# A graph network on one core: extra tiles tested ahead of the group, register words loaded early, dense product in four parts

## What is computed

```python
h = relu(layernorm(x))
# three graph convolutions, edges and self loops, norm = dinv[src] * dinv[dst]
for W, b in ((W1, b1), (W2, b2), (W3, b3)):
    h = segment_sum((h @ W)[src] * norm, dst) + b     # relu after the first two
x = x + h
h = relu(layernorm(x))
filt = edge_attr_50 @ W_rad.T + b_rad
x = x + silu(segment_sum((h @ W_pre.T + b_pre)[src] * filt, dst) @ W_post.T + b_post)
```

## Time and profile before

| | us |
|---|---|
| median of 3 runs | 6268.11 (6235.98 to 6292.54) |
| profiled execution, its own time | 6264.8 |
| its span, first to last instruction | 6263.0 |
| mean granted TensorE clock | 0.803 |

### The profile page before, as it was taken

The page is one execution under the profiler, slowest core; times in us unless marked ns, Lnnn a source line. Parts: engine busy times, 40 slices in busy tenths (PEclk is TensorE's granted clock), DMA queues, the critical chain, the costliest instruction groups (busy, mean ns, idle before and its releaser), DMA issues.

```text
span 6263.0 us, 114127 instructions
## 1 busy us (share of the span) xinstructions
PE 4667.6 (75%) x31388; PEld 3424.1 (55%) x31389; DVE 3181.7 (51%) x8799; ACT 951.1 (15%) x2182; POOL 2930.3 (47%) x3027
## 2 busy tenths in 40 slices
PE   6955787888888888599975999656666666666665
PEld 4741233444444445588855888455555555555555
DVE  6757777777766665544445444362222222222225
ACT  0010123333334554100001000010000000000002
POOL 0002123344440000276653766517777777777772
PEclk9967899999999999699967999666666666666665
DMA  1000011111121111255522555302222222222221
GB/s 32 0 15 13 27 41 43 55 55 56 56 66 52 52 63 53 71 168 168 173 55 71 168 169 175 77 29 47 47 46 47 47 46 47 46 47 46 47 47 33
DMA packets 158567, 406.28 MB, mean 65 GB/s; under 512 B 67564, under 2 KB 80940, under 8 KB 139124
## 3 DMA queue, kind: packets, MB, share of 16 engines
q1 hardware_dynamic: 62068, 305.32, 13.7%
q0 software_dynamic: 96256, 98.76, 8.5%
HBM read 307.53 MB, written 96.33 MB: 64 GB/s over the span
## 4 chain that ended last, share of the span: by engine, by line
PE 36%; POOL 25%; issue 18%; DVE 13%; DVEq 7%; DMA 1%; ACT 0%; SPq 0%; POOLq 0%; ACTq 0%
POOL rows_flat L508 25%; PE ps L1251 13%; PE ps L1343 5%; PE ps L1317 5%; PE ps L1223 4%; DVE sumT L961 4%; PE ps L1354 3%; PE ps L1240 3%; PE ps L1238 2%; DVE stage_fn L689 1%; PE ps L1209 1%; DVE hot L683 1%; DVEq L689 1%; DVEq L712 1%; DVE hot L1189 1%
## 5 line engine op out<-in xcount | busy, mean ns | idle before, releaser
L508 POOL DMA_INDIRECT rows_flat<-table,row_stage x3008 | 2917.2, 970 | 2136.9 <-issue 1844.2
L1231 PE MATMUL ps<-hot,msg_flat 128*64 128x160 f32 x3136 | 814.2, 447 | 711.2 <-DVE msg_flat L785 711.2
L1343 PE MATMUL ps<-sumT,stage_fn 128*128 128x392 f16 x3976 | 980.4, 358 | 418.1 <-DVE sumT L961 234.4
L1231 PEld LDWEIGHTS ps<-hot,msg_flat 128*64 128x64 f32 x3136 | 653.7, 216 | 827.0 <-issue 703.4
L961 DVE TENSOR_SCALAR sumT<-stage_fn,sub_start,sumT 128x784 f16<-128x784 f16 x1988 | 891.5, 481 | 0.0
L1343 PEld LDWEIGHTS ps<-sumT,stage_fn 128*128 128x128 f16 x3976 | 287.8, 101 | 1086.6 <-issue 829.4
L585 ACT ACTIVATE ring<-ps 128x784 fp8e4<-128x784 f32 x800 | 658.5, 823 | 1255.5 <-PE ps L1343 1250.0
L1251 PE MATMUL ps<-wide,ring 128*128 128x192 bf16 x9800 | 828.5, 247 | 0.0
L1251 PEld LDWEIGHTS ps<-wide,ring 128*128 128x128 fp8e4 x9800 | 805.7, 98 | 8.5
L683 DVE TENSOR_SCALAR hot<-iota,dst_rel 128x160 f32<-128x160 f32 (+1 forms) x3008 | 636.1, 287 | 226.7 <-issue 223.4
L785 DVE TENSOR_TENSOR msg_flat<-rows_flat,ps 128x512 f32<-128x512 f32 x196 | 134.6, 687 | 1007.1 <-DMA rows_flat<-table,row_stage 988.9
(11 more groups left out here) (160 smaller groups left out, 3071.1 us busy)
## 6 DMA issues: line engine op xcount, KB each, us to landing
ring<-counts SPq DMA_DIRECT2D x100, 1568.0 KB
counts<-ring SPq DMA_DIRECT2D x50, 1568.0 KB, 5.2
rows_flat<-table,row_stage POOLq DMA_INDIRECT x3008
ring<-in_radial SPq DMA_DIRECT2D x196, 200.0 KB
table<-node SPq DMA_DIRECT2D x56, 224.0 KB, 1.9
out<-node SPq DMA_DIRECT2D x13, 224.0 KB
ring<-in_dst SPq DMA_DIRECT2D x1, 784.0 KB
ring<-in_src SPq DMA_DIRECT2D x1, 784.0 KB
```

Source lines behind the costliest of these rows:

```text
L508: nc.gpsimd.indirect_dma_start(out=rows[:, j, k * D:(k + 1) * D], out_offset=None, in_=table[:, :], in_offset=bass.IndirectOffsetOnAxis(ap ...
L1231: s = nc.tensor.matmul(to, of, mats[:, k, :], start=(k == 0), stop=(k == BLOCK_TILES - 1))
L1343: m = nc.tensor.matmul(to[:, c, :], sources[:, :, k], joint[k][:, c * (JOINT // 2):(c + 1) * (JOINT // 2)], start=first, stop=True, skip_g ...
```

## The change

In `subs` the test for extra tiles moves ahead of the group. On DVE both tests now lie inside one `If(n > 0)`. On PE `If(n > 0)` comes ahead of the set's waits and matmuls; its true branch has the main tiles with the extra ones between them, its else branch has the main tiles alone, four matmuls in a row. The words t0 and n of four sets lie side by side in one table, so that DVE loads eight words at once and PE four; the load for the next group is issued ahead of the group's last set, and the first group's before the loop. The table has eight words more at its end, set to zero. PE's inner loop of two is written out, and the dense product is cut into four parts (25, 25, 24 and 24 matmuls), one behind each call of `subs`.

```diff
-        sub_tile = sbuf("sub_tile", [1, SUBS], I32)
-        sub_more = sbuf("sub_more", [1, SUBS], I32)
+        sub_table = sbuf("sub_table", [1, 2 * (SUBS + SETS)], I32)
+        by_sets = sub_table[:, 0:2 * SUBS].rearrange("a (s two k) -> a s two k", two=2, k=SETS)
+        sub_tile, sub_more = by_sets[:, :, 0, :], by_sets[:, :, 1, :]
...
+            nc.gpsimd.memset(sub_table[:, 2 * SUBS:], 0).then_inc(consts_made, 1)
...
             def subs(s4):
-                dve.load(tile_regs, sub_tile[0:1, bass.ds(s4 * SETS, SETS)])
-                dve.load(more_regs, sub_more[0:1, bass.ds(s4 * SETS, SETS)])
                 for a in range(SETS):
                     sub = s4 * SETS + a
                     t0 = counted(tile_regs[a], EDGES // P)
                     n = counted(more_regs[a], TILES // EXTRA)
+                    if a == SETS - 1:
+
+                        dve.load(tile_regs + more_regs, sub_table[0:1, bass.ds((s4 + 1) * (2 * SETS), 2 * SETS)])
 
                     dve.wait_ge(main_used, s4 * SETS + (a + 1))
...
-                    with dve.If(n > 1):
-                        with dve.Fori(0, n >> 1) as m2:
-                            for b in range(2):
-                                extra_hots(b, sub, extra_tile(t0, m2 * 2 + b))
-                    with dve.If((n & 1) > 0):
-                        extra_hots(0, sub, extra_tile(t0, n - 1))
+                    with dve.If(n > 0):
+                        with dve.If(n > 1):
+                            with dve.Fori(0, n >> 1) as m2:
+                                for b in range(2):
+                                    extra_hots(b, sub, extra_tile(t0, m2 * 2 + b))
+                        with dve.If((n & 1) > 0):
+                            extra_hots(0, sub, extra_tile(t0, n - 1))
...
+            dve.load(tile_regs + more_regs, sub_table[0:1, 0:2 * SETS])
             build_and_first_layer()
...
+            cuts = [0, 25, 50, 74, WINDOWS]
+
             def dense_part(i, h, part):
...
-                for q in range(part * (WINDOWS // 2), (part + 1) * (WINDOWS // 2)):
+                for q in range(cuts[part], cuts[part + 1]):
...
-                if part == 1:
+                if part == 3:
                     d.then_inc(dense_ready, 1)
...
             def subs(s4):
-                pe.load(more_regs, sub_more[0:1, bass.ds(s4 * SETS, SETS)])
                 for a in range(SETS):
...
+                    if a == SETS - 1:
+
+                        pe.load(more_regs, sub_table[0:1, bass.ds((s4 + 1) * (2 * SETS) + SETS, SETS)])
                     to = ps_count[a % 2]
-                    pe.wait_ge(sub_copied, s4 * SETS + (a + 1))
-                    pe.wait_ge(main_ready, s4 * SETS + (a + 1))
-                    pe.sem_inc(pe_turn, 1)
-                    for k in range(MAIN - 1):
-                        joint_tile(to, src_main[a], joint_main[a], k, k == 0)
-                    with pe.If(n > 1):
-                        with pe.Fori(0, n >> 1):
-                            for b in range(2):
-                                extra_tiles(to, b)
-                    with pe.If((n & 1) > 0):
-                        extra_tiles(to, 0)
-                    joint_tile(to, src_main[a], joint_main[a], MAIN - 1, False).then_inc(main_used, 1)
+
+                    def main_begins():
+                        pe.wait_ge(sub_copied, s4 * SETS + (a + 1))
+                        pe.wait_ge(main_ready, s4 * SETS + (a + 1))
+                        pe.sem_inc(pe_turn, 1)
+                        for k in range(MAIN - 1):
+                            joint_tile(to, src_main[a], joint_main[a], k, k == 0)
+
+                    def main_ends():
+                        joint_tile(to, src_main[a], joint_main[a], MAIN - 1, False).then_inc(main_used, 1)
+
+                    with pe.If(n > 0):
+                        main_begins()
+                        with pe.If(n > 1):
+                            with pe.Fori(0, n >> 1):
+                                for b in range(2):
+                                    extra_tiles(to, b)
+                        with pe.If((n & 1) > 0):
+                            extra_tiles(to, 0)
+                        main_ends()
+                    with pe.Else():
+                        main_begins()
+                        main_ends()
 
             def build_and_first_layer():
                 at = Pass(pe, FUSED)
                 with pe.Fori(0, PAIRS) as i:
                     for j in range(SLOTS):
-                        with pe.Fori(0, P // SUB // SETS // 2) as q:
-                            subs(i * (2 * P // SUB // SETS) + j * (P // SUB // SETS // 2) + q)
-                        if j < 2:
-                            with pe.If(i > 0):
-                                dense_part(earlier(i), 1, j)
-                        else:
-                            dense_part(i, 0, j - 2)
+                        for q in range(2):
+                            subs(i * (2 * P // SUB // SETS) + (j * 2 + q))
+                            if j < 2:
+                                with pe.If(i > 0):
+                                    dense_part(earlier(i), 1, j * 2 + q)
+                            else:
+                                dense_part(i, 0, (j - 2) * 2 + q)
...
+            pe.load(more_regs, sub_table[0:1, SETS:2 * SETS])
             build_and_first_layer()
```

More of the change, by code:

```diff
@@ L65 @@
 EPS = 1e-5
-assert BLOCKS % SLOTS == 0 and SUB * WINDOWS <= STRIDE and (P // SUB) % SETS == 0 and WINDOWS % GROUP == 0 and GROUPS % 2 == 0 and HEAD % 2 == 0
+assert BLOCKS % SLOTS == 0 and SUB * WINDOWS <= STRIDE and (P // SUB) % SETS == 0 and WINDOWS % GROUP == 0 and GROUPS % 2 == 0 and HEAD % 2 == 0 and P // SUB // SETS == 4
 def PROJECT(p):
@@ L297, in gnn_program @@
         N_LOADS = 4 + 5 + 5 + 2
-        N_CONSTS = 9
+        N_CONSTS = 10
         def groups(g, n=1):
@@ L919, in _, with sets_of @@
             settle()
+            def sets_of(subs):
+                return subs.rearrange("a (s k) -> a s k", k=SETS)
             def shifted(to, of):
@@ L924, in shifted @@
                 settle()
-                then(nc.vector.tensor_single_scalar(to, sub_i, 7, ALU.logical_shift_right))
+                then(nc.vector.tensor_single_scalar(to, sets_of(sub_i), 7, ALU.logical_shift_right))
                 settle()
@@ L929, in _ @@
             settle()
-            shifted(sub_tile[:, :], sub_tmp)
+            shifted(sub_tile, sub_tmp)
             then(nc.vector.tensor_scalar(sub_tmp, sub_end, -1.0, 0.0, ALU.add, ALU.max))
             settle()
-            shifted(sub_more[:, :], sub_tmp)
-            then(nc.vector.tensor_tensor(sub_tmp, sub_more[:, :], sub_tile[:, :], ALU.subtract))
+            shifted(sub_more, sub_tmp)
+            then(nc.vector.tensor_tensor(sets_of(sub_tmp), sub_more, sub_tile, ALU.subtract))
             settle()
@@ L941, in _ @@
             settle()
-            nc.vector.tensor_single_scalar(sub_more[:, :], sub_i, EXTRA.bit_length() - 1,
+            nc.vector.tensor_single_scalar(sub_more, sets_of(sub_i), EXTRA.bit_length() - 1,
                                            ALU.logical_shift_right).then_inc(sub_ready, 1)
@@ L1389, in build_and_first_layer @@
                     for j in range(SLOTS):
-                        with pe.Fori(0, P // SUB // SETS // 2) as q:
-                            subs(i * (2 * P // SUB // SETS) + j * (P // SUB // SETS // 2) + q)
-                        if j < 2:
-                            with pe.If(i > 0):
-                                dense_part(earlier(i), 1, j)
-                        else:
-                            dense_part(i, 0, j - 2)
+                        for q in range(2):
[5 more added lines that the diff above has]
+                                dense_part(i, 0, (j - 2) * 2 + q)
                         with pe.If(i < at.rounds):
                             split_block(at, i, j, ps_more_fused[j % 2])
-                for part in range(2):
+                for part in range(4):
                     dense_part(PAIRS - 1, 1, part)
```

## The result

The changed kernel takes 6361.39 us, median of 4 runs (6306.49 to 6364.28), against 6267.69 for the kernel before in the same comparison (median of 4, 6235.98 to 6292.54). The ratio, taken over all runs and so not exactly the quotient of the two medians, is 1.0139 with a 95% interval of 1.0075 to 1.0202: slower by some 1.4%, where 6122 was forecast. The profiled execution took 6306.49 (span 6304.7), 41.7 us more than the one of before, though its joined stage is 53 us shorter.

The account below looks back on a forecast made before the run. A chain between engines was taken as the bound: DVE in the first fifteen pairs, PE and ACT's turn in the last ten. Gains of 80 + 63 = 143 us from 6264.8 gave 6122, range 6050 to 6205.

Parts of the forecast that it names:

- PE's fetch: Pair loop's branch back: PE's longer body is read anew each pass, counted 1.0 us in last ten, 0.7 in first fifteen.
- the load in the gap: DVE between groups, first fifteen pairs: the early load removes 0.82 us for each of 120 groups, less 8 us.
- the dense product in four parts: Last ten pairs: dense parts of 2.1 us let ACT empty both buffers; 48.0 us a pass before PE's fetch.
- Stages after 2463 must keep their length: Code behind the joined stage, not edited, was to take as long as before: 0 us.
- the rest of the last dense part covers it: Branch back: PE's queue arrives while most of the 2.1 us dense part still runs, leaving 1.0 us of stall.
- DVE's own stall: Branch back of the pair loop: DVE's 3.44 us stall was to come at nearly the same place as PE's.
- Rival C: Pair loop's branch back: PE's fetch paid in full, 25 x 4.0 = 100 us instead of 20, total 6202; chance 0.14.
- Rival E: Pair loop: PE, reading its body anew, runs dry at many places, 375 us instead of 20, about 6480; chance 0.07.
- The test ahead: Sets of the pair loop: PE and ACT's turn of two sets falls from 2.41 to 2.02 us; DVE gains nothing.
- the steady state: Last ten pairs: a group of four sets with its dense part takes 5.85 us, eight groups 46.8.

Follow-up runs that it names:

- e2: The kernel before with 12 never executed DVE instructions behind the joined stage, so only later code moves: 6356.01 us, ratio 1.0166.
- e1: The changed kernel with 116 never executed DVE instructions behind the joined stage, putting later code 128 behind its place of before: 6245.67 us, ratio 0.9981.
- e3: e1 with PE's inner loop of two kept as a loop, dense product still in four parts: 6146.67 us, ratio 0.9829.
- e4: The kernel before with the early load of eight words (four on PE) and its table alone: 6239.87 us, ratio 0.9972.
- e12: The changed kernel with dense product in two parts, PE's inner loop kept, DVE's later code 128 behind its place of before: 6098.16 us, ratio 0.9704.
- e9: The kernel before with the test ahead, loads in the gap, two dense parts, DVE's later code 128 further on: 6203.88 us, ratio 0.9882.
- e10: e5 with 112 instead of 116 never executed DVE instructions, so layer 3's loop stands as in e3: 6217.85 us, ratio 0.9884.
- e5: e3 with the loads back in the gap between groups, which leaves DVE's later code four instructions further on: 6306.73 us, ratio 1.0088.
- e13: The kernel before with 2 never executed DVE instructions behind the joined stage: one execution, 6435 us.
- e8: e3 with four times 190 jumped-over instructions in PE's pair loop, body 2,299 instead of 1,539: 6370.71 us, ratio 1.0183.
- e7: e3 with four times 102 jumped-over instructions in PE's pair loop, body 1,947 instead of 1,539: 6195.04 us, ratio 0.991.

## Why the prediction was wrong, and where it was right

The profiled execution stands 184.5 us above the forecast (6306.5 against 6122). By the table above: 89.7 from layer 3's loop, 53.3 from the last ten pairs, 37.0 from the first fifteen, 5.3 from the rest, less 0.6 for the two clock steps that cancel; together 184.7. The sign came from a term put at nothing, the time of the code behind the stage. Within the stage, which gained 52.7 of the 143, the terms that failed are PE's fetch, the load in the gap and the dense product in four parts.

- **"Stages after 2463 must keep their length"** is the step that failed, and it changed the sign. The prediction treated code that isn't changed as unmoved. e2 makes the loss without the change, e1 takes it away with the change in place. The hint stood in the earlier trace rows: DVE's code is fetched in pieces of 8 KB while it runs, so the place of a loop can matter; I used the row for the length of PE's body alone. Without this the changed kernel is e1, which can't be told from the kernel before.
- **PE's fetch, last ten pairs: counted 1.0 a pass, it costs 5.5** (e1 544.3 less e3 489.2, in ten). In the first fifteen it costs 13.3 in all, where 10 were counted, though the branch takes longer there (5.1 to 7.0 us): there most of the stall is hidden, as forecast. That the body would be read anew in each pass was right (2,301 instructions, forecast about 2,250), and the price for the whole pause, 3.4 to 4, was of the size of the branch's 5.17, if low. Wrong for the last ten was the assumption that the rest of the last dense part covers it. PE's queue reaches the branch (2167.53) 1 us after its last part began (2166.51), so little more than 1 us of a stall of 5.07 is hidden. DVE's own stall does not lie beside it, as the prediction had it, but ahead of it: DVE stands at its branch from 2162.6 to 2165.5, PE from 2167.5 to 2172.6. Behind PE's stall come a second wait, for DVE, and matmuls at the lower clock. Rival C had this mechanism; as it kept the other terms, it gave 6202. Rival E, many dry places in the pass, is not seen.
- **The load in the gap: 0.82 x 120 less 8 = 90 in the first fifteen.** Alone it gives 34.5 (e4), beside the test ahead 68.3 (e12 against e9), and 50.2 with four parts (e3 against e10). That the two edits need each other I had not seen. Why they do is argued, not shown: in e4 PE waits 48.6 us less for DVE's tiles than before (157.1 against 205.7), but 36.5 us more with nothing in front of it but its own queue, where its tests lie; with the test ahead (e12) that wait is short. First fifteen pairs, before, e4 and e12:

```profile
PE ps L1343 <- issue: 69.7, 272, 1.3
PE ps L1352 <- issue: 106.2, 303, 3.6
PE ps L1353 <- issue: 19.5, 67, 0.8
```

  In the last ten passes the early load gives 10.6 (two parts, e12 against e9) or takes 9.5 (four parts, e3 against e10), where 0 was forecast. In both pairs DVE's branches back take some 23 us more with the load early, so what the load itself is worth there is not shown. The eight words take 0.60 us in the median, where I chose 0.40:

```profile
L1040 DVEq TENSOR_LOAD <-sub_table x200: 594/603/1855, 554.2 to 2379.2; - x100
```

- **The test ahead: nothing in the first fifteen, the most in the last ten.** Last ten 65.7 beside the early load (e12 against e4), the most of any part, as forecast in kind; alone 50.9 (e9), beside 28.8 us less at DVE's branch back. First fifteen 22.8 alone and 56.6 beside the early load (e12 against e4), where I gave DVE nothing; that makes up for the load's shortfall, so that e12 gains 91 there and the sum of 90 looks right for a wrong reason.
- **The dense product in four parts** was to hide ACT's turn behind a shorter dense part. With the early load it gives 1.7 in the last ten and costs 36.5 in the first fifteen (e3 against e12); with the loads in the gap it gives 21.8 and costs 18.4 (e10 against e9). In all it loses 34.8 in the one case and gains 3.4 in the other. Its forecast for the steady state was right (5.7 to 5.8 us a group, 48.9 a pass in e3, whose PE fetches nothing, against 48.0 forecast without the fetch), but the test ahead with the early load reaches nearly that in two parts, 49.1 (e12). So beside the early load the gain was counted for the part that did not bring it.

Not settled: where the median's excess comes from beyond the profile. 6361.4 less 6267.7 is 93.7, and the stages give 42 in the profiled execution, whose own time was the lowest of the changed kernel's; its other executions lie 54 us and more above it. e2, with nothing but the moved code, lies 91 above its kernel before (6356.0 against 6265.4), little more than the 87.0 of its layer 3 loop. The excess is likely two more of the clock steps below, which come in this size, but the other executions have no trace.

## What to carry to other kernels

Count the instructions that a change adds to each engine and look at every loop behind it, not only at those that it edits: the instruction queues' packet counts in the page (here 217 to 287) tell at once whether a loop is read anew, and moving later code by never executed instructions tests it. A written-out loop costs what the fetch at its branch back costs: by stage e1, written out, is 68.4 us slower than e3, which keeps the loop. Measure parts of a change in pairs, with and without each other, before saying which one pays; here the best kernel (ratio 0.9704) is the change less one of its three parts, with a short body and its later code put back in place. Before a ratio of this size is read, take the steps of the clock out stage by stage: the same kernel gave 0.9836 and 0.9704.

## What the runs showed of the hardware

- **Place of DVE's code.** A loop of 282 instructions that ran through its 12 passes with one piece fetched, fetched 61 pieces of 8 KB in them when it stood 2, 4 or 12 instructions further on, and took 83, 80 and 87 us longer. Of the 89.7 that the changed kernel lost, 36.7 are more busy time of PE (583.98 against 547.30, granted clock 0.93 instead of 1.00) and 53 are idle.
- **PE's code.** A body of 1,539 instructions is kept, one of 1,947 read anew in part, one of 2,299 or 2,301 wholly. The Trainium skill, "Runtime: NRT & Kernel Launch", section "Instruction fetch mechanics", gives 2048 instructions for PE; the trace at 2,301 agrees, but at 1,947 the fetches have begun.
- **The clock in four stretches.** In four stretches the kept traces show one of two lengths, about 30 us apart, for the same instructions: the start to the joined stage (500 or 530 us), from the joined stage to layer 2 (171 or 201), between layers 2 and 3 (235 or 265) and behind layer 3's loop (226 or 256). The steps go with no variant. Behind layer 3, for example, the long form stands in the changed kernel, e5 and e13, whose loop was slow, but also in e8, e10 and e12, whose loop was not, and not in e2. The step at the start, before and then after:

```profile
350.00:412.00 62.00, 2.83 (x32) 2.58 (x32) 51.84 (x54) 0.57 (x2) 0.00 (x0) 0.56 0.00 0
412.00:485.00 73.00, 67.01 (x294) 57.64 (x294) 12.64 (x15) 19.87 (x32) 0.39 (x1) 0.50 0.11 41
```

```profile
350.00:412.00 62.00, 2.83 (x32) 2.58 (x32) 51.88 (x52) 0.57 (x2) 0.00 (x0) 1.00 0.00 0
412.00:455.00 43.00, 37.63 (x294) 33.55 (x294) 12.40 (x15) 19.89 (x32) 0.00 (x0) 0.98 0.18 70
```

  PE did the same in both up to here: it was busy for 96 of the 100 us before 350, then for 2.8 us, then idle for 63.5. In the kernel before the granted clock fell to the lower level (1.2 GHz) in the idle time and stayed there for the 294 matmuls behind it; after, it stayed at the higher (2.4 GHz). No run tells why. Behind layer 3's loop 150.04 against 120.74 us of matmuls is the step (granted clock 0.51 against 0.59), and between layers 2 and 3 it appears in e7 (265.1 us against 234.6). From the joined stage to layer 2, before and then e1:

```profile
2463.30:2634.20 170.90, 98.62 (x668) 90.11 (x665) 95.03 (x152) 36.66 (x54) 36.06 (x33) 0.66 0.15 54
```

```profile
2413.90:2614.00 200.10, 125.93 (x648) 112.81 (x645) 94.58 (x152) 36.57 (x54) 36.07 (x33) 0.55 0.13 46
```

  Whoever compares two single executions of this kernel has to take these steps out first.
- **DVE's branch back** costs 2.8 to 6.6 us in a pass, by variant and pass (table above), but next to nothing in the last ten passes of e5, e9 and e10 (0.00 to 0.15 us in eight of them), whose body is 842 instructions long and begins at 137, where e3's has 837 and begins at 138. No run tells why.
